# Cross attention of a Perceiver block on one core: the set-up in another order

## The reference

```python
def reference(x, ctx_512, ...):
    x = x + _L0_xattn_ref(_layernorm(x), ctx_512, Wq, Wkv, Wo)     # the part that changes
    x = x + _L0_attn_ref(_layernorm(x), wq, w_down, wk_up, wv_up, wo)
    x = x + _L0_ffn_ref(_layernorm(x), Wr, W1, W2, W3)             # 8 experts, top 2
    return x

def _L0_xattn_ref(x, z, Wq, Wkv, Wo):          # 16 heads of 32
    Q = (x @ Wq.T).reshape(B, xN, 16, 32)
    KV = (z @ Wkv.T).reshape(B, zN, 2, 16, 32)
    K, V = KV[:, :, 0], KV[:, :, 1]
    attn = softmax(einsum('bqhd,bkhd->bhqk', Q, K) * 32 ** -0.5)
    O = einsum('bhqk,bkhd->bqhd', attn, V).reshape(B, xN, 512)
    return O @ Wo.T
```

## Time and profile before

| | |
|---|---|
| median of 3 runs | 1572.47 us (1572.13 to 1577.39) |
| the profiled execution | 1574.53 us, its span 1572.8 us |
| TensorE busy | 1457.5 us, 93% of the span |
| VectorE, ScalarE, GpSimd busy | 69%, 52%, 34% |
| mean granted TensorE clock | 0.966 of full speed |

### The profile page before, as it was taken

How to read it: one execution, slowest core, us unless ns; L and a number is a source line. 1 busy time by engine, 2 the same in 40 slices (tenths; PEclk the granted TensorE clock), 3 DMA queues, 4 the chain that set the end, 5 groups by cost and what they waited for, 6 DMA issues and landing times. The chain is left out here.

```text
span 1572.8 us, 39406 instructions
## 1 busy us (share of the span) xinstructions
PE 1457.5 (93%) x14912; PEld 1301.5 (83%) x14912; DVE 1082.3 (69%) x1935; ACT 811.9 (52%) x1527; POOL 542.3 (34%) x816
## 2 busy tenths in 40 slices
PE   6899989898989989997899998779999999999997
PEld 5888878787878878885777776678999999999996
DVE  2677767575766767664567676578878778787784
ACT  3666656565666656654443433244545555555552
POOL 1222212121222212221776777443333323333332
PEclk8999999999999999998999999879999999999999
DMA  7111100010110100100011114146878778777871
GB/s 282 61 28 29 29 23 28 23 27 23 28 29 22 28 23 28 29 15 1 9 36 36 36 37 150 56 141 223 293 258 281 253 267 271 253 266 251 288 246 41
DMA packets 130778, 174.83 MB, mean 111 GB/s; under 512 B 16953, under 2 KB 89337, under 8 KB 130626
## 3 DMA queue, kind: packets, MB, share of 16 engines
q1 hardware_dynamic: 120242, 145.56, 28.5%
q0 software_dynamic: 10384, 27.05, 4.7%
HBM read 157.18 MB, written 19.06 MB: 112 GB/s over the span
## 5 line engine op out<-in xcount | busy, mean ns | idle before, releaser
L2042 DVE TENSOR_TENSOR lo<-raw,hi 128x1024 fp32r<-128x1024 f32 x207 | 246.0, 1219 | 7.7 <-ACT hi L1978 6.4
L52 PE MATMUL mo_bank<-xT_hi,hi 128*128 128x256 f32 x768 | 216.5, 282 | 3.0 <-DVE xT_lo L2051 2.8
L54 PE MATMUL mo_bank<-xT_lo,hi 128*128 128x256 f32 x768 | 215.3, 280 | 0.0
L53 PE MATMUL mo_bank<-xT_hi,lo 128*128 128x256 f32 x768 | 215.2, 280 | 0.0
L1978 ACT CAST hi<-raw 128x1024 fp32r<-128x1024 f32 x207 | 208.3, 1048 | 6.3 <-DMA raw<-in_L_ffn_W_dram 4.3
L564 ACT ACTIVATE Pr<-xa_s,nmax 128x257 f32<-128x257 f32 x256 | 119.1, 473 | 160.5 <-DVE nmax L658 160.4
L1998 ACT ACTIVATE sl<-mo_bank 128x256 f32<-128x256 f32 x117 | 45.0, 385 | 245.9 <-PE mo_bank L54 245.9
L52 PE MATMUL xa_s<-zT_hi,QK_hi 128*128 128x258 f32 x512 | 156.8, 306 | 11.2 <-issue 9.3
L53 PE MATMUL xa_s<-zT_hi,QK_lo 128*128 128x258 f32 x512 | 149.3, 292 | 16.8 <-issue 16.8
L52 PEld LDWEIGHTS mo_bank<-xT_hi,hi 128*128 128x128 f32 x768 | 144.9, 189 | 9.8 <-issue 5.4
L54 PE MATMUL xa_s<-zT_lo,QK_hi 128*128 128x258 f32 x512 | 149.9, 293 | 0.0
(11 more groups left out here) (303 smaller groups left out, 3923.8 us busy)
## 6 DMA issues: line engine op xcount, KB each, us to landing
raw<-in_L_ffn_W_dram SPq DMA_DIRECT2D x207, 512.0 KB, 5.8
raw<-in_ctx_dram SPq DMA_DIRECT2D x64, 256.0 KB, 2.6
out_dram<-x_res SPq DMA_DIRECT2D x16, 256.0 KB
xs<-xn SPq DMA_DIRECT2D x16, 256.0 KB, 2.2
x_res<-in_x_dram SPq DMA_DIRECT2D x1, 3840.0 KB, 18.8
VL<-v_last_rows SPq DMA_DIRECT2D x128, 2.0 KB, 1.5
raw_o<-in_L_xattn_Wo_dram SPq DMA_DIRECT2D x1, 1024.0 KB, 5.4
raw_q<-in_L_xattn_Wq_dram SPq DMA_DIRECT2D x1, 1024.0 KB, 8.6
```

What stands on the lines that cost most here:

```text
L52: pe.matmul(out, lh, rh, start=start, stop=False)
L53: pe.matmul(out, ll, rh, start=False, stop=False)
L54: return pe.matmul(out, lh, rl, start=False, stop=stop)
L2042: vW.done(dve.tensor_tensor(lo, raw, hi.bitcast(F32), ALU.subtract), f"p{c}{q}")
```

## The change

Six things change in the order of work; nothing is computed otherwise.

1. SP loads tiles 0 and 1 of x first (512 KB instead of 256), and the four first context batches inside the set-up, behind Wk and ahead of the other 14 tiles of x.
2. Tile 0 is turned (`turn_x`) and copied (`x_out`) inside the set-up, between the jobs of Wv and those of Wq; tile 1 is normalised there too, as VectorE's last work (with `rstd_of` on GpSimd).
3. The values of the last keys leave the set-up: TensorE makes them behind the projection of tile 1, into `bank_u`; the round over DRAM is issued by SP in the main block.
4. The copies of QK of tile 0 are split between ScalarE (two heads of each group) and VectorE (the other two).
5. The projection of tile 1 is cut into its halves, one between the two pairs of `absorb_k`, one behind.
6. TensorE makes 8 products `ident` x `ident` ahead of its wait for the last keys, and 8 more ahead of its wait for Wo.

```diff
-                    sp.dma_start(x_res[:, 0, :], xt[:, 0, :]).then_inc(x_first, 16)
+                    sp.dma_start(x_res[:, 0:2, :], xt[:, 0:2, :]).then_inc(x_first, 16)
...
-                    sp.dma_start(x_res[:, 1:, :], xt[:, 1:, :]).then_inc(x_rest, 16)
-                    sp.wait_ge(hi_done, len(jobs) + 1)
-                    sp.dma_start(vlast_dram[0], vl_hi[:].bitcast(F32)).then_inc(vl_put, 16)
-                    sp.wait_ge(lo_done, n_split + 1)
-                    sp.dma_start(vlast_dram[1], vl_lo[:].bitcast(F32)).then_inc(vl_put, 16)
+                    for j in range(BT):
+                        load_z(sp, j, j)
+                    sp.dma_start(x_res[:, 2:, :], xt[:, 2:, :]).then_inc(x_rest, 16)
                     sp.wait_ge(k_loaded, 16)
...
+                    rstd_of(pool, 1)
                     pool.wait_ge(zeroed, 1)
...
+                    def warm(n):
+                        for _ in range(n):
+                            pe.matmul(bank_z[:, 0:P], ident[:], ident[:], start=True, stop=True)
+
                     for n, (load, blocks, _dst, width) in enumerate(jobs):
+                        if n < 2:
+                            warm(8)
                         pe.wait_ge(loaded[load], 16)
...
-                    pe.wait_ge(hi_done, n_values)
-                    for k in range(KL):
-                        mm = pe.matmul(bank_o[0:B, :], zl[:, k, :], WvT[:, k, :], start=(k == 0), stop=(k == KL - 1))
-                    mm.then_inc(turned, 1)
+                        if n == n_values - 1:
+                            turn_x(pe, 0)
...
-                    act.wait_ge(turned, len(jobs) + 1)
-                    act.copy(vl_hi[:], bank_o[0:B, :]).then_inc(hi_done, 1)
+                        if n == n_values - 1:
+                            x_out(act, 0)
...
-                    dve.wait_ge(hi_done, len(jobs) + 1)
-                    dve.tensor_tensor(vl_lo[:], bank_o[0:B, :], vl_hi[:].bitcast(F32), ALU.subtract).then_inc(lo_done, 1)
-                    dve.wait_ge(lo_done, n_split + 1)
+                    statistics(dve, 1)
+                    normalise(dve, 1)
+                    dve.wait_ge(lo_done, n_split)
...
                     if first:
+                        beside(sp)
+                        for n, half in enumerate((vl_hi, vl_lo)):
+                            sp.wait_ge(vl_split, n + 1)
+                            sp.dma_start(vlast_dram[n], half[:].bitcast(F32)).then_inc(vl_put, 16)
                         sp.wait_ge(vl_put, 32)
...
-                turn_x(0)
                 project_q(0, 0)
                 project_q(0, 1, False)
                 turn_z(0, 0, 0)
                 pe.wait_ge(a_Q, 2)
-                turn_x(1)
-                for m in range(NQ):
-                    need(pe, a_QK, m - m % 2)
-                    absorb_k(Qp[0], m)
+                turn_x(pe, 1)
+                absorb_k(Qp[0], 0)
+                absorb_k(Qp[0], 1)
                 project_q(1, 0)
+                pe.wait_ge(a_QK, 2)
+                pe.wait_ge(d_QK, 2)
+                absorb_k(Qp[0], 2)
+                absorb_k(Qp[0], 3)
                 project_q(1, 1, False)
+                for k in range(KL):
+                    mm = pe.matmul(bank_u[0:B, 0, :], zl[:, k, :], WvT[:, k, :], start=(k == 0), stop=(k == KL - 1))
+                mm.then_inc(vl_made, 1)
                 pe.wait_ge(a_QK, NQ)
+                pe.wait_ge(d_QK, NQ)
...
+                        if first and j == 1:
+                            pe.wait_ge(vl_split, 2)
                         if some:
                             gather_z(s - 1)
...
                 for m in range(NQ):
-                    qk_out(m, 0, m)
+                    act.wait_ge(pe_QK, m - m % 2 + 2)
+                    qk_heads(act.copy, m, 0).then_inc(a_QK, 1)
+                act.wait_ge(d_QK, NQ)
                 qk_hi(0, 0, 0, NQ)
                 q_out(1, 1, (0, 1))
+                act.wait_ge(vl_made, 1)
+                act.copy(vl_hi[:], bank_u[0:B, 0, :]).then_inc(vl_split, 1)
...
-                dve.wait_ge(x_rest, 16)
-                statistics(dve, 1)
-                normalise(dve, 1)
                 z_lo(0)
+                for m in range(NQ):
+                    dve.wait_ge(pe_QK, m - m % 2 + 2)
+                    qk_heads(dve.tensor_copy, m, 2).then_inc(d_QK, 1)
                 qk_lo(0, 0, 0)
+                dve.wait_ge(vl_split, 1)
+                dve.tensor_tensor(vl_lo[:], bank_u[0:B, 0, :], vl_hi[:].bitcast(F32), ALU.subtract).then_inc(vl_split, 1)
```

More of the change, by code:

```diff
@@ L120, in cross_attention @@
         vl_put = sem("vl_put")
+        zl = sb("zl", [P, KL, B])
         zT_hi, zT_lo = sb("zT_hi", [P, KL, KW], F32R), sb("zT_lo", [P, KL, KW], F32R)
@@ L135, in cross_attention, with load_z, turn_x, x_out @@
         x_first, x_rest = sem("x_first"), sem("x_rest")
-        pe_X = sem("pe_X")
+        pe_X, a_X = sem("pe_X"), sem("a_X")
+        z_in = [spare.w13[:, j // 2, 2 * (j % 2):2 * (j % 2) + 2, :] for j in range(BT)]
+        z_got = [sem(f"z_got{j}") for j in range(BT)]
+        def load_z(sp, s, j):
+            sp.dma_start(z_in[j], ctx_in[s, 0:LAST, :].rearrange("(p c) l -> p c l", c=CH)).then_inc(z_got[j], 16)
+        def turn_x(pe, i):
+            pe.wait_ge(v_ln, LN * i + 4)
+            for k in range(KC):
+                mm = pe.transpose(bank_o[:, k * P:(k + 1) * P], xn[:, k * P:(k + 1) * P], ident[:])
+            mm.then_inc(pe_X, 1)
+        def x_out(act, i):
+            act.wait_ge(pe_X, i + 1)
+            act.copy(xnT.rearrange("p k q -> p (k q)"), bank_o[:]).then_inc(a_X, 1)
         def statistics(dve, i):
@@ L169, in cross_attention @@
             raw_zl = sbs("raw_zl", [B, L])
-            zl = sbs("zl", [P, KL, B])
             loaded = [setup.enter_context(nc.semaphore(f"w_loaded{i}")) for i in range(4)]
@@ L265, in _ @@
                     dve.tensor_copy(key_of[:], own_key[:]).then_inc(masked, 1)
-                    dve.wait_ge(hi_done, len(jobs) + 1)
-                    dve.tensor_tensor(vl_lo[:], bank_o[0:B, :], vl_hi[:].bitcast(F32), ALU.subtract).then_inc(lo_done, 1)
-                    dve.wait_ge(lo_done, n_split + 1)
+                    statistics(dve, 1)
+                    normalise(dve, 1)
+                    dve.wait_ge(lo_done, n_split)
                     dve.wait_ge(masked, 3 + BT)
-        z_in = [spare.w13[:, j // 2, 2 * (j % 2):2 * (j % 2) + 2, :] for j in range(BT)]
         Qp = [spare.w2[:, u, :] for u in range(2)]
@@ L286, in cross_attention @@
         rinv = sb("rinv", [P, NQ])
-        z_got = [sem(f"z_got{j}") for j in range(BT)]
-        vl_got = sem("vl_got")
+        vl_got, vl_made, vl_split = sem("vl_got"), sem("vl_made"), sem("vl_split")
         pe_T, pe_S, pe_PT, pe_U, pe_QK = (sem(n) for n in ("pe_T", "pe_S", "pe_PT", "pe_U", "pe_QK"))
@@ L294, in cross_attention @@
         a_T, a_E, a_PT, a_QK, a_QKh, U_out = (sem(n) for n in ("a_T", "a_E", "a_PT", "a_QK", "a_QKh", "U_out"))
-        a_X, a_Q, a_OT = (sem(n) for n in ("a_X", "a_Q", "a_OT"))
+        a_Q, a_OT, d_QK = (sem(n) for n in ("a_Q", "a_OT", "d_QK"))
         v_T, v_QK, v_mx, v_N, v_PT = (sem(n) for n in ("v_T", "v_QK", "v_mx", "v_N", "v_PT"))
@@ L300, in cross_attention, with qk_heads @@
         s_end = BT * n_tile
+        def qk_heads(copy, m, hh):
+            at, two = (m % 2) * KL * P, slice(hh, hh + 2)
+            return copy(QK[0][:, :, 4 * m + hh:4 * m + hh + 2, :].rearrange("p k h t -> p h k t"),
+                        bank_s[:, two, at:at + KL * P].rearrange("p h (k t) -> p h k t", k=KL))
         def by_pair(eng, tile):
@@ L332, in tile @@
                         s = BT * i + j
[L333 to L338, removed]
+                        if not first:
+                            sp.wait_ge(pe_T, s - BT + 1)
+                            sp.wait_ge(g_Z, s - BT + 1)
+                            load_z(sp, s, j)
                     if first:
+                        beside(sp)
+                        for n, half in enumerate((vl_hi, vl_lo)):
+                            sp.wait_ge(vl_split, n + 1)
+                            sp.dma_start(vlast_dram[n], half[:].bitcast(F32)).then_inc(vl_put, 16)
                         sp.wait_ge(vl_put, 32)
@@ L355, in turn_z @@
                     mm.then_inc(pe_T, 1)
[L357 to L361, removed]
                 def project_q(i, half, wait_first=True):
@@ L475, in tile @@
                             need(pe, v_OP, i)
-                            turn_x(i + 2)
+                            turn_x(pe, i + 2)
                         if not (last and j == BT - 1):
@@ L508, in z_hi @@
                     act.copy(zT_hi[:, :, 0:LAST], bank_z[:].rearrange("p (k q) -> p k q", k=KL)).then_inc(a_T, 1)
-                def x_out(i):
-                    act.wait_ge(pe_X, i + 1)
-                    act.copy(xnT.rearrange("p k q -> p (k q)"), bank_o[:]).then_inc(a_X, 1)
                 def q_out(i, slot, halves):
```

(14 more changed lines are left out.)

## The result

The changed kernel takes 1527.82 us (median of 4 runs, 1525.57 to 1531.04) against 1572.3 (median of 4, 1566.78 to 1577.39): 44.5 us less, ratio 0.9719, 95% interval 0.968 to 0.9759. I had forecast 1565.7, range 1562.5 to 1571. The direction was right; the size was six and a half times the 6.8 us that I gave, and about 37 of the 44.5 us come from a place that I had set aside as unchanged.

A forecast was written before the change was run, and what follows sets the result against it. The prediction took the start of the first scores, at 41.17 us, as what the change could move: 4.3 (set-up) + 1.0 (first projection) + 1.5 (to the scores) = 6.8 us off the median 1572.5, giving 1565.7, range 1562.5 to 1571.

The forecast's parts named there:

- the steady part does not change: From tile 1 on: TensorE, busy 532 of 561 us, stays as it is; only an earlier start of the scores gains.
- no change: Rival, chance 0.10: scores start 5 to 7 us earlier, but later low-clock stretches eat the gain; 1571 to 1573 us.
- Products of the identity: Set-up, TensorE: both groups of 8 end before Wo lands at 11.1 us and cost nothing; Wo's transposes find full clock.
- Loads: Set-up: 256 KB more of x ahead of Wo take 0.68 us; Wo lands at 11.1, Wq at 15.3.
- End of the set-up: VectorE is last, at 18.8; with 0.66 for the barrier the first projection starts at 19.4, 4.3 us earlier.
- First projection: Behind the barrier: TensorE idles 2.0 us, one low-clock stretch follows; 5.47 us against 6.54, so 1.0 us less.
- full clock throughout: Rival, chance 0.27: the gap at the barrier leaves the clock alone; 8.3 us less, 1564.2 us.
- To the first scores: From turning tile 1 to the first scores: 8.6 to 8.7 us instead of 10.1, so 1.5 us less.
- the likeliest case: Whole kernel, chance 0.40: one low-clock stretch; 6.8 us less in sum, 1564 to 1568 us by itself.
- Low clock out of the set-up: Rival, chance 0.20: first projection runs as slowly as before; 4.6 to 5.8 us less, 1566.7 to 1567.9 us.

The follow-up runs named there:

- run 1: Kernel before with only the 16 products of the identity added in TensorE's set-up: 1540.09 us, ratio 0.9796.
- run 8: Kernel before with 16 products of one element added behind the loop, at the end of cross attention: 1575.11 us, ratio 1.0005.
- run 9: Changed kernel with the four context batches loaded behind the 14 tiles of x again: 1537.58 us, ratio 0.9786.
- run 10: Changed kernel with the projection of tile 1 whole, behind both pairs of `absorb_k`: 1531.25 us, ratio 0.9745.
- run 2: Changed kernel without the 16 products of the identity, all reordering kept: 1568.33 us, ratio 0.9981.
- run 3: Kernel before with 16 products of the identity by one column of it added at the start of the set-up: 1536.71 us, ratio 0.9774.
- run 4: Changed kernel with its 16 full products of the identity replaced by 16 of one column at the set-up's start: 1531.03 us, ratio 0.9735.
- run 7: Kernel before with 64 products of one element (256 instructions) added at the start of TensorE's set-up: 1575.71 us, ratio 1.0008.
- run 12: Kernel before with 60 products of one element (240 instructions) added at the start of TensorE's set-up: 1564.77 us, one run.
- run 6: Kernel before with 56 products of one element (224 instructions) added at the start of TensorE's set-up: 1540.57 us, ratio 0.979.
- run 5: Kernel before with 8 products of one element (32 instructions) added at the start of TensorE's set-up: 1536.52 us, ratio 0.9764.

## Why the prediction was wrong, point by point

**The step that failed** is the first: "the steady part does not change, and what the change can give is how much earlier the first scores start". It rested on TensorE's 532 of 561 us read as nearly full. The 29 us that were missing were there to be asked about. I took the clock's 0.97 in the same row for the luck of scattered gaps, gave the "no change" rival 34 us at the lower level from it, and did not look where they stood: at five jumps of a loop, every 88 us, each behind two gaps put down to "issue". 37 of the 44.5 us are this. What the runs showed in its place: the loop of the kernel before had its code brought again in each of five passes, 522.9 us for twelve tiles, and 485.6 to 486.0 in every kernel whose loop stands elsewhere.

**Products of the identity, said to lie in the wait for Wo and to cost nothing.** Right as to their work: 3.75 us and 2.57 us, done before Wo landed. What was not in the sum is that 16 products are 64 instructions ahead of a loop.

**Loads.** Wo landed at 11.25, 11.1 given. Right.

**End of the set-up.** The first projection began at 18.82, 19.4 given; 4.9 us earlier instead of 4.3. VectorE was the last, at 18.5, as said; the barrier took 0.3 and not 0.66, likely because no DMA issue stood ahead of it, which no run tried alone.

**First projection.** 3.81 us, where I took 5.47 with one low stretch. TensorE's gap across the barrier was 1.41 us and not 2.0, and the clock stayed up, as at the gap of 1.41 in the earlier trace rows. The rival "full clock throughout" (0.27) is what happened in the set-up. But the length of the gap, by which I chose between the cases, does not decide it: behind the same gap of 2.52 us the first projection took 6.54 us in the kernel before and 3.84 in runs 1 and 8, and behind 2.42 us it took 3.81 in run 9. Why the clock fell in one and not in the other stays open.

**To the first scores.** 32.06 - 23.38 = 8.68 us from turning tile 1; 8.6 to 8.7 given. Right, and run 10 shows the half projection's part of it, 1.3 us. In sum the first scores start 9.1 us earlier; I gave 6.8 for the likeliest case and 8.3 for the one that came: that mechanism and its size held.

**Of the 9.1 us, not all can be booked.** The set-up of the kernel before is itself uneven: in run 8, which does not touch it, the first scores start at 38.5, 2.7 earlier, since its two projections ran at the full clock (3.84 us each, for 6.54 and 5.47), in part made up by waits. The reordering without the products is worth 0.2% (run 2, ratio 0.9981, 0.9962 to 1.0) and 5.7 us between runs 3 and 4.

**The end.** At the last mark of cross attention the two kernels are 48.0 us apart in the profiled runs (723.0 and 675.0), at the end 44.8: 3.2 us are given back later. The low stretches lie differently there, and TensorE's waits for "issue" in self attention are 8.2 us in all before and 10.1 after; which of them costs it was not tried. The 14 profiled runs differ by 8.5 us behind that mark (845.6 to 854.1), so the 3.2 may be scatter.

**Low clock out of the set-up.** This rival (0.20) fell: 12 transposes took 1.53 us from 11.25 on, 2.82 before, and the projection at 18.82 ran at the full clock, with nothing but transposes between 10.4 and 17.4. The rule behind it (the Trainium skill, "TensorE: Matmul & The Clock Gate", section "Part 4: PE-mode transpose": transposes are no activity) is not borne out by that.

**Code was not in the working at all.** The page that I should have drawn on is the Trainium skill's "Runtime: NRT & Kernel Launch", section "Instruction fetch mechanics". It says that TensorE's instruction memory holds 2048 instructions and is filled in blocks of 256, and that a taken branch whose target lies outside the current two pages stalls for a fetch. The block of 256 agrees with runs 7 and 12 against run 6 and with the 258 of self attention. The page calls the memory a FIFO with sequential prefetch that gains nothing from locality; here the measurement decides otherwise, as 390 us of the loop ran with no packet on queue 8, jumps back among them.

## What to carry to other kernels

A loop whose code comes near to what the engine keeps can be slow or fast by its place alone, so any edit ahead of it, however small, may move the time by its whole refetch: here 44.5 us looked like the reward of a reordering, and 37 of them come with 16 to 64 further instructions of any kind. Look for "issue" gaps that come back at a loop's period, count the packets of the instruction queue in the steady part, and if there are any, pad the loop or shorten it before judging other changes. And time a reordering at a place of the loop that is fast in both kernels (here run 3 against run 4, 5.7 us), or the two effects can't be told apart.

## What the runs showed of the hardware

- Where the loop's code was brought again, the kernel before lost 6.9 to 7.9 us a pass: two gaps, of 1.6 to 2.0 and 3.2 to 3.75 us, and a stretch at half clock behind them. With the border further into the pass (run 12) the second gap was 1.6 to 2.7 us and the twelve tiles took 517.7 us instead of 522.9.
- 32 records of a one-column float32 product took 6.96 us, 218 ns each, where 16 records of 128 columns at the same point took 3.75 us, 234 ns each. The columns left out saved next to nothing; both load the same 128x128 weights. With one column of weights as well (run 5) 16 records took 0.54 us, 34 ns each.
- Behind those 7 us of one-column products Wo's transposes took 2.82 us for 12, as without any product, and 1.53 us behind the full products: the clock was not up.
- The split copies of QK did not hinder each other at the banks: two took 1.29 us on VectorE beside two in 1.07 us on ScalarE, where two such copies alone took 1.11.
